# Attention and mixture-of-experts layer on one core: ten parts carried instead of nine, the finish in seven steps, and another order in the tail

## What is computed

```python
h = layernorm(x)                                  # then attention's own layernorm, ln_w, ln_b
q, k = l2norm(heads(xn @ Wq)), l2norm(heads(xn @ Wk)); v = heads(h @ Wv)      # 16 heads of 8
m = sigmoid((q @ k.T - 0.29514) * 15) * (q @ gq)[:, None] * (k @ gk)[None, :] # no softmax
x = x + layernorm((m @ v) @ Wo + bo)
xn = layernorm(layernorm(x)) * gamma + beta
comb = normalised top 2 of softmax(xn @ router_w)                             # 8 experts
swiglu(x, gu, dn) = (silu(clip(gate, -10, 10)) * up) @ dn,   gate, up = split(x @ gu)
out = sum_e comb[:, e] * swiglu(xn, gate_up_w[e], down_w[e]) + swiglu(xn, shared...)
x = x + layernorm(out)
```

## Time and profile before

| | |
|---|---|
| median of three runs | 731.08 us |
| the profiled execution, its own time | 732.92 us |
| its span, first to last instruction | 730.2 us |
| busy: PE, ACT, DVE, POOL | 619.7, 563.5, 418.6, 164.6 us |
| blocks 0 to 3, first sigmoid of each | 37.49, 184.27, 319.54, 464.15 us |
| last rounds' values end, tail begins | about 610.7 us |
| PE's clock granted, mean of the span | 0.940 of 2.4 GHz |

### The profile page before, as it was taken

The page is one execution under the profiler, slowest core; times in us unless marked ns, Lnnn a source line. Parts: engine busy times, 40 slices in busy tenths (PEclk is TensorE's granted clock), DMA queues, the critical chain, the costliest instruction groups (busy, mean ns, idle before and its releaser), DMA issues. The chain is left out here.

```text
span 730.2 us, 15309 instructions
## 1 busy us (share of the span) xinstructions
PE 619.7 (85%) x5928; PEld 259.5 (36%) x5928; DVE 418.6 (57%) x1107; ACT 563.5 (77%) x661; POOL 164.6 (23%) x149
## 2 busy tenths in 40 slices
PE   3587999999999999998999899989998994368840
PEld 2452211112223344432334344333343442347730
DVE  6775184920653555447545855475458554648984
ACT  1579799999999899988898899888988993005520
POOL 1122000000041221100543121014431220237642
PEclk9998999999999999999999999999999998559975
DMA  8600001620044344400643354005444440158921
GB/s 325 226 30 30 30 9 19 264 104 1 9 137 128 123 142 120 142 26 6 181 151 119 122 137 143 23 23 164 144 114 120 146 138 4 40 148 267 319 69 51
DMA packets 47639, 82.02 MB, mean 112 GB/s; under 512 B 5456, under 2 KB 25168, under 8 KB 47568
## 3 DMA queue, kind: packets, MB, share of 16 engines
q1 hardware_dynamic: 45088, 76.31, 32.8%
q0 software_dynamic: 2048, 4.20, 1.9%
q10 hardware_dynamic: 432, 0.54, 0.3%
HBM read 64.59 MB, written 16.45 MB: 111 GB/s over the span
## 5 line engine op out<-in xcount | busy, mean ns | idle before, releaser
L697 ACT ACTIVATE res<-S 128x1024 f32<-128x1024 f32 x348 | 349.2, 1067 | 22.5 <-PE S L810 11.9
L824 PE MATMUL AV<-res,vg 128*8 128x512 f32 x2048 | 305.4, 599 | 1.5 <-DVE coll L1199 1.5
L697 ACT ACTIVATE res<-UO 128x1024 f32<-128x1024 f32 x164 | 175.2, 1069 | 10.6 <-PE S L810 9.7
L600 POOL TENSOR_TENSOR work<-work 128x512 f32<-128x512 f32 x64 | 81.8, 1279 | 243.9 <-DVE work L1320 243.0
L810 PE MATMUL S<-qT,kT 32*128 32x512 f16 x696 | 104.5, 387 | 2.7 <-ACT res L697 2.4
L898 PE MATMUL GB<-xT,gu_ring 128*128 128x128 f16 x1164 | 84.2, 224 | 11.1 <-DVE slot L1300 3.9
L672 ACT ACTIVATE work<-work,scl 128x512 f32<-128x512 f32 x64 | 46.8, 731 | 57.8 <-DVE work L1313 57.7
L574 POOL DMA_INDIRECT xs_dram<-xrow,slot x32 | 32.1, 1002 | 243.1 <-DVE slot L1300 235.1
L898 PEld LDWEIGHTS GB<-xT,gu_ring 128*128 128x128 f16 x1164 | 67.5, 100 | 32.6 <-issue 17.4
L810 PEld LDWEIGHTS S<-qT,kT 32*128 32x128 f16 x696 | 25.9, 91 | 146.6 <-ACT res L697 93.2
L1313 DVE TENSOR_SCALAR work<-GB,scl 128x512 f32<-128x512 f32 x56 | 45.3, 809 | 52.3 <-PE GB L898 52.1
(11 more groups left out here) (232 smaller groups left out, 662.1 us busy)
## 6 DMA issues: line engine op xcount, KB each, us to landing
gu_ring<-gu_dram SPq DMA_DIRECT2D x60, 512.0 KB, 3.4
dn_ring<-dn_dram SPq DMA_DIRECT2D x60, 256.0 KB, 2.9
work<-in_gu SPq DMA_DIRECT2D x8, 512.0 KB, 10.4
gu_dram<-gu_ring SPq DMA_DIRECT2D x8, 512.0 KB, 2.6
ys_dram<-work SPq DMA_DIRECT2D x60, 64.0 KB
work<-in_down SPq DMA_DIRECT2D x8, 256.0 KB, 11.1
dn_dram<-dn_ring SPq DMA_DIRECT2D x8, 256.0 KB, 2.9
work<-xs_dram SPq DMA_DIRECT2D x4, 448.0 KB, 4.7
```

Source lines behind the costliest of these rows:

```text
L600: nc.gpsimd.tensor_tensor(hid[u % 2], prod[u % 2], sg[u % 2], ALU.mult).then_inc(hid_ready, 1)
L697: nc.scalar.activation(res[:, k % 2, 2 * half:2 * half + 2, :].rearrange("p h t -> p (h t)"), score_banks(i, k, half).rearrange("p h t -> ...
L824: mm = nc.tensor.matmul(AV[32 * j:32 * j + HD, :], vg[:, s, G * g + j, :], res[:, k % 2, j, :], start=s == 0, stop=s == ST - 1)
```

## The change

1. The table. Parts start at round 23 instead of 22. Ten parts are carried: the up product of unit 13 to round 5, the others to rounds 12 to 20 (before: 10, 12 to 19). The shared unit's parts go to rounds 21, 21, 22 (before 17, 21, 20). The DVE work of the part in round 5 stands inside `attention_out`, after its second statistics; a new semaphore `proj_read` lets that matmul begin once DVE has read the projection from GB.
2. After the ranks, PE waits for `place_ready` (L1296's result) instead of `slot_ready`. DVE's split of the shared input (`shared_in`) moves from round 11 to 13.
3. `finish` has seven steps, at rounds 37, 38, 40, 41, 43, 44, 46; the reciprocal root is cut in two.
4. Tail, order. The outputs of units 13 to 15 of experts 3 leave the carried parts; they stand among units 0 to 2 of experts 4, in banks OB and AV. The high halves of units 14 and 15 are made by ACT.
5. Tail, SP's queue. Five tiles' weights, then the tiles' rows, then the saves of experts 3, each followed by one more tile's weights; the saves of the last experts start beside the weights of tile 10. Six more places for gate and up weights (in `kT` and `res`) and four for down weights (in `vg`), which attention no longer needs.
6. POOL in blocks 2 and 3 issues scatters 4 to 7 together, before the last product of the carried parts.

```diff
-FINISH_ROUND = 36
-FIRST_PART, LAST_PART = 22, 60
-CARRIED = (10, 12, 13, 14, 15, 16, 17, 18, 19)
-SHARED_PARTS = {0: 17, 2: 20, 1: 21}
+FINISH_ROUNDS = (37, 38, 40, 41, 43, 44, 46)
+FIRST_PART, LAST_PART = 23, 60
+CARRIED = (5, 12, 13, 14, 15, 16, 17, 18, 19, 20)
+SPLIT_SHARED_ROUND = 13
+SHARED_PARTS = {0: 21, 1: 21, 2: 22}
...
+        def place_of(i, t, ring, loaded, more, extra, first):
+            if late(i) and first <= t < first + len(more):
+                return more[t - first], extra[t - first], 16
+            m = (i - 1) * NT + (t - len(more) if late(i) and t >= first else t)
+            return ring[:, m % len(loaded), :], loaded[m % len(loaded)], (m // len(loaded) + 1) * 16
...
                 sp.wait_ge(tile_ready, i)
+                if late(i):
+                    for t in range(5):
+                        load_weights(i, t)
+                    for n in range(3):
+                        load_tiles(i, n)
+                    for t in range(5):
+                        save_y(i - 1, NT - 5 + t)
+                        load_weights(i, 5 + t)
+                    for t in range(10, NT):
+                        load_weights(i, t)
+                        save_y(i, t - 10)
+                    for t in range(5, NT):
+                        save_y(i, t)
+                    return
...
                         if k == RANK_ROUND:
                             rank(i, readers)
-                            readers = [(slot_ready, i)]
+                            readers = [(place_ready, i)]
...
             project_last(NB)
+            readers = unit_part(NB - 1, *CARRIED_PARTS[0], [(proj_read, NB)])
+            free(readers)
             turn_tokens(NB)
             route(NB)
             rank(NB, [(diff_ready, NB)])
-            readers = [(slot_ready, NB)]
-            for u, part in CARRIED_PARTS:
+            readers = [(place_ready, NB)]
+            for u, part in CARRIED_PARTS[1:-LAG]:
                 readers = unit_part(NB - 1, u, part, readers)
             for u in range(NU):
                 n = (NB - 1) * NU + u
                 gate(NB, u, readers if u == 0 else [(gate_clipped, n - 1)] if u >= 2 else [])
-                if u >= LAG:
+                if u == 0:
+                    up(NB, u, [])
+                if u < LAG:
+                    late_out(NB - 1, NU - LAG + u)
+                else:
                     late_out(NB, u - LAG)
-                if u > 0:
-                    turn_tiles(NB, u, [])
-                up(NB, u, ...)
-                if u == 0:
-                    turn_tiles(NB, u, [])
+                turn_tiles(NB, u, [])
+                if u > 0:
+                    up(NB, u, ...)
...
                 stats(link, lambda j: x1[i % 2][:, j, :])
+                if i > 1:
+                    unit_part(i - 1, *CARRIED_PARTS[0])
                 variance(link, s_var, 0, SUB, True)
...
+                    if late(i) and u < LAG:
+                        outputs(i - 1, NU - LAG + u)
+                    elif late(i):
+                        outputs(i, u - LAG)
+                    if late(i) and u < 2:
+                        hidden_low(i - 1, NU - 2 + u)
+                    elif 2 <= u < NU + 2:
                         hidden_low(i, u - 2)
```

More of the change, by code:

```diff
@@ L286, in build @@
         dn_loaded = [sem(f"dn_loaded{n}") for n in range(DS)]
+        gu_extra = [sem(f"gu_extra{n}") for n in range(len(gu_more))]
+        dn_extra = [sem(f"dn_extra{n}") for n in range(len(dn_more))]
         y_ready = sem("y_ready")
@@ L346, in y_bank, with high_by_act, reader_of, gu_place @@
         def y_bank(i, u):
[L348 removed]
+            return ((OB if u % 2 else AV[:]) if late(i) or (i == NB - 1 and u >= NU - LAG) else GB[:])[:, 0:D]
         def tile_bank(i, t):
             return S[:, 2 + t % 2, :].bitcast(F16)[:, 0:2 * P] if late(i) else GB[:].bitcast(F16)[:, (2 + t % 2) * 2 * P:(3 + t % 2) * 2 * P]
+        def high_by_act(i, u):
+            return late(i) or i == NB - 1 and u >= NU - 2
+        def place_of(i, t, ring, loaded, more, extra, first):
[3 more added lines that the diff above has]
+            return ring[:, m % len(loaded), :], loaded[m % len(loaded)], (m // len(loaded) + 1) * 16
+        def reader_of(i, t, depth, more, first):
+            if late(i) and first <= t < first + len(more):
+                return 0
+            v = (t - len(more) if late(i) and t >= first else t) - depth
+            if v < 0:
+                i, v = i - 1, v + NT
+            elif late(i) and v >= first:
+                v += len(more)
+            return (i - 1) * NU + v + 2 if i > 0 else 0
+        def gu_place(i, t):
+            return place_of(i, t, gu_ring, gu_loaded, gu_more, gu_extra, 1)
+        def dn_place(i, t):
+            return place_of(i, t, dn_ring, dn_loaded, dn_more, dn_extra, 0)
         def turned_with(u):
@@ L543, in _ @@
                     residual(i + 1)
-            for t in range(NT - 5, NT):
-                save_y(NB, t)
             save_result(NB - 1)
@@ L1324, in hidden_low @@
                 n = (i - 1) * NU + u
-                if not late(i):
+                if not high_by_act(i, u):
                     dve.wait_ge(hid_ready, n + 1)
@@ L1368, in unit_part @@
                             outputs(i, u - LAG)
-                    if 2 <= u < NU + 2:
+                    if late(i) and u < LAG:
[5 more added lines that the diff above has]
+                    elif 2 <= u < NU + 2:
                         hidden_low(i, u - 2)
-                    if u == LAG or u > LAG and late(i):
+                    if u == LAG and not late(i):
                         outputs(i, u - LAG)
@@ L1485, in rounds @@
                             places(i, link)
+                        for j, u, part in parts_in(i, k):
+                            if k != CARRIED[0]:
+                                unit_part(j, u, part)
+                        if k == SPLIT_SHARED_ROUND:
                             shared_in(i)
-                        for j, u, part in parts_in(i, k):
-                            unit_part(j, u, part)
                     else:
@@ L1503, in rounds @@
                         gates(i, GATE_ROUNDS.index(k))
-                    if i > 1 and FINISH_ROUND <= k < FINISH_ROUND + 6:
-                        finish(i - 1, link, k - FINISH_ROUND)
+                    if i > 1 and k in FINISH_ROUNDS:
+                        finish(i - 1, link, FINISH_ROUNDS.index(k))
             rounds(0, False)
@@ L1516, in _ @@
             places(NB, link)
-            shared_in(NB)
-            for u, part in CARRIED_PARTS:
+            for u, part in CARRIED_PARTS[1:-LAG]:
                 unit_part(NB - 1, u, part)
+                if u == NU - 2 and part == 0:
+                    shared_in(NB)
             for u in range(NU):
@@ L1525, in _ @@
             for i in (NB - 1, NB):
-                for step in range(6):
+                for step in range(7):
                     finish(i, link, step)
```

83 lines of the change are left out of this document (48 added, 35 removed).

## The result

| | before | after |
|---|---|---|
| median | 730.98 us (729.35 to 734.54, 10 runs) | 726.68 us (723.37 to 728.67, 10 runs) |
| ratio, 95% interval | | 0.9946 (0.993 to 0.9962) |
| profiled execution, its span | 732.92, 730.2 us | 728.29, 726.5 us |
| start of block 1, then lengths of blocks 1, 2, 3 | 184.27; 135.27, 144.61, 145.42 | 184.72; 135.26, 141.55, 141.47 |
| tail, last sigmoid's end to the end of the span | 120.68 | 123.50 |

The lengths are distances between the first sigmoids of two blocks; block 3's ends with its last sigmoid.

The account below looks back on a forecast made before the run. PE and ACT were busiest but kept waiting, with VectorE the bound from clip 4 on. Terms 5.0 + 2.4 + 4.7 = 12.1 us took the profiled execution from 732.92 to 720.8, median 719.0 us; range 713.5 to 726.

Parts of the forecast that it names:

- Carried parts: Rounds 10 to 22 of blocks 2 and 3: most waits go, 29.7 us each; 5.0 us gained over all blocks.
- us of waits: Rounds 10 to 22: time above 27.4 us, the price of bare rounds and parts; 4.6 in block 2, 5.9 in block 3.
- The tenth part in round 5: Blocks 2 and 3: costs 0.25 us each; VectorE's 0.75 us for it is hidden in attention_out by 1.48 us of slack.
- The loss of 0.35 in block 1: Block 1: one part less (0.25) against new waits in rounds 21 and 22 (0.6), a loss of 0.35 us.
- Finish in seven steps: Rounds 36 to 42 of blocks 2 and 3: spreading the steps gains 1.2 us in each block, 2.4 us in all.
- Tail, up to the shared unit: Tail's start: the shared gate starts at 647.1 instead of 654.99, 7.9 us earlier.
- tile rows: Tail: rows asked for by 644.8 instead of 652.41; turning at 651.2 instead of 657.53, 6.3 us earlier.
- units 1 to 3: Tail: added outputs and a low half cost 1.4 to 1.9 us; clip 4 at 662.7, 4.7 us gained (ends 3 and 6).
- More weight places give nothing: Tail behind clip 4, bound by VectorE: no gain; late saves need 0.43 us of queue each and catch up.
- D: Rival: tail's rows come no earlier behind five tiles' weights, tail gain gone, 723.7 us, some 722 for a delay between; chance 0.14.
- E: Rival: slower, PE at half clock through the tail's units, 1.9 us lost per unit, 747 if all fifteen; chance 0.04.

Follow-up runs that it names:

- seven-step kernel: The kernel before, with finish in seven steps at rounds 37 to 46, the root in two, and nothing else: 725.43 us.
- rounds-alone kernel: The kernel before with the new table, wait for place, split in round 13, seven steps and scatters; old SP queue, weight places and tail order: 725.88 us.
- the kernel with three tiles ahead: The changed kernel with own semaphore and later gathers, and three tiles' weights instead of five ahead of the tiles' rows: 717.39 us.
- both edits: The changed kernel with an own semaphore for the last five saves of experts 3 and GpSimd's gathers five products later: 717.03 us.

## Why the prediction was wrong

**Carried parts, 5.0 us.** The stretch of rounds 10 to 22 was sized well: 30.2 us for 29.7, with the wait at `place` at 1.42, inside its bounds. But 1.25 us of the 5.9 "us of waits" counted for block 3 were not the table's. The same instructions took 31.99 in another kernel; in the profile of before the clock was 0.60 from 489 to 493 behind a wait, and one execution was read as the rule, though the 0.95 in the row had been noticed. So the 7.0 us of blocks 2 and 3 agree with the 7.4 forecast partly by luck. The tenth part in round 5, "hidden" by 1.48 us of slack, cost 0.42 and 0.80: in block 3 it brought 2.3 us into the chain instead of 0.75. Against the seven-step kernel, block 2 of the rounds-alone kernel is 1.5 us shorter and block 3 0.95 (143.04 to 141.55, 142.41 to 141.46), so the term is 2.4 us and not 5.0, and 1.8 of them go again in the tail of the rounds-alone kernel. The loss of 0.35 in block 1 did not come (135.26 for 135.27).

**Finish in seven steps, 2.4 us.** Right in direction and mechanism; 3.3 measured, in one profile of each kernel.

**Tail, up to the shared unit; tile rows; units 1 to 3, 4.7 us.** Clip 4 came as forecast (662.3 for 662.7), though the steps on the way did not; their errors offset each other. The shared gate was at 649.1 on the old clock (642.53 + 6.57) and not at 647.1. One of these 2.0 us arose ahead of the first part, which came at 634.9 (628.34 + 6.57) and not at 633.9: the tenth part's 0.75 us stand in `attention_out` here too, and behind them the first step of the root took 1.25 us beside GpSimd's product (614.24), as in round 5. The other arose at VectorE's high half, which took 2.04 us beside GpSimd's product and 0.92 in the kernel before:

```profile
644.66 0.92 DVE L1330 CAST hid_hi<-work 128x512 f16<-128x512 f32 x1
```

The turning came at 652.9 on that clock, where 651.2 was forecast. From clip 1 to clip 4 took 7.75 us, where 7.53 plus 1.4 to 1.9 had been counted, and that made up for it. The rows were asked for at 650.4. The prediction had the last scatter issued by 644.8 and up to 4.7 us of its landing hidden; SyncE waited for that landing until 5.3 us behind the last issue, which the weights delay, as the kernel with three tiles ahead shows. In the changed kernel nobody waited for the rows all the same, since TensorE was late too; in two of the later kernels it did (1.65 and 3.87 us). The Trainium skill, "SBUF — State Buffer", section "SBUF: two separate sides", has the rule for the high half and for the root's first step, in round 5 and in the tail: not only instructions with two SBUF inputs lock out GpSimd's, as the prediction quoted it, but also one-input ones in the two-port mode. The trace agrees with that half of it too: a shift of four numbers took 0.17 or 1.27, a cast 0.42 or 2.04, and beside GpSimd's product they ended 0.03 and 0.30 us behind its end. In which mode they ran no row shows, nor what held the cast before the product's recorded start (639.52), 0.47 us after its own.

**The step that failed:** "More weight places give nothing in the stretch that VectorE bounds; the late saves need 0.43 us of queue each and catch up in the last three units." It counted the saves' issue time and only the saves of the last experts. It did not ask who waits for the saves of experts 3. In the kernel before, the last of them was issued at 654.96 and its first reader, GpSimd's first gather, came at 662.95, 8 us later:

```profile
654.96 0.32 SPq L490 DMA_DIRECT2D ys_dram<-work  x1
...
662.95 1.28 POOL L588 DMA_INDIRECT y_tok<-ys_dram,slot  x1
```

In the changed kernel, on the same clock, the reader is there at 658.3 (660.24 - 8.55 + 6.57), 4.7 sooner, since the units start sooner; the issue is at 661.3, 6.3 later, since the outputs stand among the units and the saves among the weights; and the landing is 5.3 behind the issue, since the new weight places let SyncE fill the queue ahead of it. From clip 4 to the end of the span took 62.88 us before (730.2 less 667.32) and 70.74 now, 7.86 more: 7.56 for the stall (10.37 for 2.81), 0.95 for the half clock in the next unit (3.77 for 2.82), 1.78 for the last unit's weights (4.59 for 2.81), less 1.62 for eight units that ran faster and 0.81 at the end. The kernels without the stall have their medians at 717.0 to 719.3, and 719.0 was predicted. That nearness is partly luck as well: with both edits the tail is 7.0 us shorter than before (113.71 for 120.68) where 4.7 was forecast, which makes up for the carried parts.

**The rivals.** None was this one. D was nearest, a landing behind weights on one queue; but it was about the rows, and they were in time. E's half clock came, as a consequence and for one unit. The rule that D cites from the Trainium skill, "DMA: Bandwidth & Descriptors", "Queues, rings and completion order" (transfers of one issuing queue are consumed in ring order), fits what the runs show of the saves: 1.8 us from issue to reader with nothing ahead, 5.3 behind weights. The prediction had applied it to the one transfer that it was thinking of.

## What to carry to other kernels

When a queue's order changes, list for every transfer in it, not only for those that the change is about, who waits for its landing, when it was needed before and when it will be; here 8 us of slack were gone when the reader moved 5 us forward and the issue 6 us back. A semaphore that counts a whole group makes the first reader wait for the last member; and an in-order queue on another engine (here GpSimd's gathers in front of its products) turns one late landing into two waits, so that removing either alone gives half or nothing. A part put into a serial chain costs what it slows behind it too: 0.75 us became 2.3. Compare stretches with the same instructions in several blocks or executions before pricing a wait: a lapse of the clock behind a wait looks like a wait.

## What the hardware showed beyond that

- The price of a wait of TensorE is not its length. 2.14 us of idling in round 12 cost 2.3 us more than 1.42 us did, with the clock at 0.63 in the 4 us behind it. And it is not the same each time: behind 1.4 us of idling at the same place the clock stayed at 1.00 in 19 of 20 stretches and fell to 0.62 in one.
- Identical instructions before block 1 took from 181.8 to 184.7 us in the thirteen profiles of this study, most of the difference in rounds 0 to 9 of block 0 (42.4 to 44.9 us); a change of a few us is better read from the stretch it touches than from medians of four runs.
- Weights on SyncE's queue also slowed GpSimd's scatters, which have a queue of their own: 5.3 us from the last issue to its reader with five tiles' weights asked for (DMA share 1.01 and 404 GB/s over these 5.3 us), 2.7 with three (0.61 and 234 GB/s).
